# Fourier stage of a four-layer stack: other ticks for widenings, filters, back transforms and output products

## The reference

```python
x = einsum('bchw,oc->bohw', x, w_in)            # 64 -> 384 channels
xf = rfft2(8x8 patches of x) * fft_filter
x = irfft2(xf)                                  # back to pixels
x = depthwise_conv3x3(x, w_dw, padding=1)       # 9 taps per channel
x1, x2 = split(x, 2, axis=1)
x = einsum('bchw,oc->bohw', gelu(x1) * x2, w_out)   # 192 -> 64 channels
```

## Time and profile before

| | |
|---|---|
| median of three runs | 21086.46 us (21080.1 to 21098.46) |
| profiled execution, its own time | 21098.81 us |
| span of the profiled execution | 21097.0 us |
| first filter of the Fourier stage | 17206.8 us |
| last filter of the Fourier stage | 20572.2 us |
| busy in the span: VectorE, GpSimd, TensorE, ScalarE | 92%, 73%, 71%, 54% |

### The profile page before, as it was taken

One profiled execution on the slowest core, in us unless ns is written; L12 is line 12 of the kernel. 1 busy time (PEld: TensorE's weight loads), 2 busy tenths in 40 slices (PEclk: granted clock), 3 DMA queues, 4 the chain that ended last, 5 costly groups with the idle time before them and its releaser, 6 DMA issues. The chain is left out here.

```text
span 21097.0 us, 183109 instructions
## 1 busy us (share of the span) xinstructions
PE 14907.7 (71%) x47074; PEld 5387.9 (26%) x47074; DVE 19421.3 (92%) x12666; ACT 11474.3 (54%) x12716; POOL 15394.4 (73%) x6584
## 2 busy tenths in 40 slices
PE   4876666666666666666666666666666668888885
PEld 2331222222222222222222222222222224444444
DVE  5778999999999999999999999999999978888886
ACT  1115555555555555555555555555555546666663
POOL 3766777777777777777777777777777758888881
PEclk8887777777777777777777777777777779999997
DMA  3224444444444444444444444444444421111113
GB/s 117 95 90 112 111 114 116 111 113 116 114 109 116 115 112 114 115 112 112 114 117 110 114 116 110 114 116 114 109 116 114 111 63 30 30 30 30 30 26 132
DMA packets 574458, 2089.44 MB, mean 99 GB/s; under 512 B 70785, under 2 KB 88051, under 8 KB 550067
## 3 DMA queue, kind: packets, MB, share of 16 engines
q1 hardware_dynamic: 569122, 2081.45, 39.6%
q10 hardware_dynamic: 5265, 7.14, 0.1%
HBM read 856.39 MB, written 158.18 MB: 48 GB/s over the span
## 5 line engine op out<-in xcount | busy, mean ns | idle before, releaser
L1287 POOL TENSOR_TENSOR prod<-h,c_bc 128x1024 f32<-128x1024 f32 x4096 | 9571.1, 2350 | 4069.1 <-PE py L992 3088.1
L1246 DVE TENSOR_TENSOR_SCAN h<-da,state,px 128x1024 f32<-128x1024 f32 x4096 | 9613.4, 2347 | 193.2 <-DVE px L1239 24.6
L1133 ACT ACTIVATE da<-d_bc,a_neg 128x1024 f32<-128x1024 f32 x4096 | 4666.6, 1145 | 4670.2 <-DVE h L1246 4644.1
L1239 DVE TENSOR_TENSOR px<-px,du_bc 128x1024 f32<-128x1024 f32 x4096 | 5046.0, 1232 | 359.6 <-PE px L925 141.2
L925 PE MATMUL px<-cf,bsel 32*128 32x512 f32 x4096 | 3113.4, 899 | 3199.0 <-DVE h L1246 3198.9
L992 PE MATMUL py<-prod,ysel 128*32 128x512 f32 x16384 | 2725.9, 798 | 1560.0 <-POOL prod L1287 1560.0
L1874 POOL TENSOR_TENSOR acc<-acc,ta 128x1024 f32<-128x1024 f32 (+1 forms) x1040 | 2424.7, 2339 | 499.7 <-DVE acc L1774 370.1
L925 PEld LDWEIGHTS px<-cf,bsel 32*128 32x128 f32 x4096 | 957.5, 257 | 4989.4 <-DVE h L1246 4037.7
L1774 DVE SCALAR_TENSOR_TENSOR p_c<-zb,w_dw,p_c 128x1024 f32<-128x1024 f32 (+1 forms) x1560 | 1987.3, 1274 | 42.3 <-PE p_c L1546 9.8
L992 PEld LDWEIGHTS py<-prod,ysel 128*32 128x32 f32 x16384 | 511.2, 132 | 3808.6 <-POOL prod L1287 2800.9
L1673 ACT ACTIVATE ta<-zb,w_dw 128x1024 f32<-128x1024 f32 (+1 forms) x1040 | 1168.5, 1128 | 297.1 <-POOL acc L1874 275.5
(11 more groups left out here) (219 smaller groups left out, 18319.6 us busy)
## 6 DMA issues: line engine op xcount, KB each, us to landing
d_bc<-delta SPq DMA_DIRECT2D x1024, 512.0 KB, 8.1
du_bc<-du SPq DMA_DIRECT2D x1024, 512.0 KB, 7.7
c_bc<-c_rows_dram SPq DMA_DIRECT2D x1024, 512.0 KB, 4.0
hx<-x_dram SPq DMA_DIRECT2D x252, 256.5 KB, 4.8
st_x<-in_x_dram SPq DMA_DIRECT2D x32, 1024.0 KB, 4.8
ax<-in_x_dram SPq DMA_DIRECT2D x64, 512.0 KB, 3.4
xr<-x_dram SPq DMA_DIRECT2D x64, 512.0 KB, 6.0
x_dram<-xo SPq DMA_DIRECT2D x64, 512.0 KB, 5.3
```

What stands on the lines that cost most here:

```text
L1133: nc.scalar.activation(da[n % 4][:, :], d_bc[:, n % J, :], ACT.Exp, scale=a_neg[t.l][:, n:n + 1]).then_inc(da_done, 1)
L1239: nc.vector.tensor_tensor(out=x[:, :], in0=px[q % 2][:, :], in1=du_bc[:, j, :], op=ALU.mult).then_inc(m1_done, 1)
L1246: nc.vector.tensor_tensor_scan(h[:, n % 8, :], da[n % 4][:, :], x[:, :], state[:, 2 * t.l + t.b, n:n + 1], ALU.mult, ALU.add).then_inc(sca ...
L1287: nc.gpsimd.tensor_tensor(out=prod[j][:, :], in0=h[:, n % 8, :], in1=c_bc[q % 2][:, :], op=ALU.mult).then_inc(m2_done, 1)
```

## The change

The diff changes tick tables and the place of a few calls; no instruction is added or left out, and no wait is added or removed by hand.

```diff
--- before.py
+++ after.py
@@ -1426,14 +1426,14 @@
         TICKS = 24
         CONV_AT = {4 * (u - 1) + 1: u for u in range(1, 6)}
         NEXT_AT = 21
-        PROJECT_AT = (1, 4)
-        WIDEN_AT = {2 * p + 1: p for p in range(NP)}
-        BACK_AT = {j + 3: j for j in range(NJ)}
+        PROJECT_AT = (2, 5)
+        WIDEN_AT = {2 * p - 1: p for p in range(1, NP)}
+        BACK_AT = {j + 2: j for j in range(NJ)}
         TURN_AT = {4 * g + 7: g for g in range(NG)}
         FREQ_AT = {4 * g + 9: g for g in range(NG)}
-        CARRY_AT, GELU_BACK_AT, GELU_AT = 1, 5, 17
-        FILTER_N = {n: p for p, n in enumerate((3, 5, 8, 10, 13, 15, 18, 20))}
-        RESIDUAL_N, STATS_N = (3, 7), (4, 8)
+        CARRY_AT, GELU_BACK_AT, GELU_AT = 1, 6, 17
+        FILTER_N = {n: p for p, n in enumerate((1, 3, 6, 8, 11, 13, 16, 18))}
+        RESIDUAL_N, STATS_N = (5, 9), (6, 10)
 
         @block.sync
         def _(eng):
@@ -1582,8 +1582,6 @@
                 for j in range(TICKS):
                     if j in CONV_AT:
                         conv(s, b, CONV_AT[j])
-                    if not first and j in PROJECT_AT:
-                        project(s - 1, nb, r if rows_left else None, PROJECT_AT.index(j))
                     if not no_next:
                         if j in WIDEN_AT:
                             widen(ns, r + b, nb, WIDEN_AT[j])
@@ -1591,6 +1589,10 @@
                             from_freq(ns, BACK_AT[j])
                         if j == NEXT_AT:
                             conv(ns, nb, 0)
+                            if not no_row:
+                                widen(s + 2, r + 1, b, 0)
+                    if not first and j in PROJECT_AT:
+                        project(s - 1, nb, r if rows_left else None, PROJECT_AT.index(j))
                     if b == 0 and not no_row:
                         if j in TURN_AT:
                             turn(r + 1, TURN_AT[j])
@@ -1605,6 +1607,7 @@
                 for j in range(2 * p, 2 * p + 2):
                     from_freq(0, j)
             conv(0, 0, 0)
+            widen(1, 0, 1, 0)
             slot(0, 0, 0, first=True)
             slot(0, 1, 1)
             with pe.Fori(1, NR - 1) as r:
```

## The result

The changed kernel takes 21477.17 us (median of 4; 21474.63 to 21486.73) against 21090.99 for the kernel before: a ratio of 1.0184 (95% interval 1.0167 to 1.0202), +386 us. The forecast had the direction (+195) and not the size; 21477 lies 37 us above its range. The profiled execution took 21475.12.

What follows compares the result with a forecast made beforehand. VectorE was taken to set the pace, losing time to its filters' waits. Slots of 58.2 and 53.9 us make 112.1 against 105.8, +6.3 times 31 = +195, hence about 21280 us; range 21120 to 21440.

Steps and rivals of the forecast that it cites:

- walk: Step-by-step timing of two slots in the steady stage: 112.1 us against 105.8, +195 us in all; chance 0.6.
- T: VectorE's first tap of a slot, from which the forecast counts its times.
- wait for conv 5: End of the b = 0 slot: conv 5 ends at 51.6 for a VectorE ready at 51.3.
- Part 1: Widening 0 ahead: filter 0's wait goes (3.9 and 1.3); filter 1 waits 0.95 in b = 0.
- Part 2: Next wait lands at filter 3: T + 17.3 in b = 0, 16.9 in b = 1.
- Part 3: Projects later: TensorE idles 2.8 us behind project 1 for gelu and placement 3; filter 4 7.4 behind filter 3.
- part 4: Filters 5 to 7 by pitches: 5.0 and 8.2 us in b = 1; 5.9, 4.85 and 5.9 in b = 0.
- new buffer wait: Filter 3 also waits for back transform 3, behind its widening in the same tick: about 0.95 us a time.
- Half clock again: Rival: TensorE's clock falls behind the 2.8 us idle in each slot; 2.4 lost each, +149, 21430 us; chance 0.15.
- GpSimd's 22.3 us chain: From the end of unit 3 to GpSimd's first sum of unit 5, 22.3 us; placement 1 hangs on it.
- The stall is hidden: Rival: back transform 4 does not wait for the gelu; 2.8 less a slot, 21110 us, no change; chance 0.12.
- faster: Rival: about 3 us less in each slot's chain to filter 3, stall hidden too; -150, 20935 us; chance 0.13.

Runs made afterwards that it cites:

- e1: Changed kernel with three quarters of conv 2 repeated behind project 1, where TensorE idles for placement 3: 21312.24 us (ratio 1.0108 to the kernel before).
- e4: Kernel before with the early widening 0 alone, at tick 21 of the slot ahead: 20990.79 us (ratio 0.9954).
- e2: Changed kernel with ScalarE's late gelu one tick later (GELU_BACK_AT 6 becomes 7): 21246.16 us (ratio 1.0075 to the kernel before).
- e6: Kernel before with only the projects' part of the change (projects, late gelu, residuals and statistics later): 21421.91 us (ratio 1.0155).
- e5: Changed kernel with four buffers v instead of two: 21416.03 us (ratio 1.0154 to the kernel before).
- e3: Changed kernel with projects, late gelu, residuals and statistics back where they were before: 21079.95 us (ratio 0.9997 to the kernel before).

## Why the prediction was wrong

**Its walk held.** Step by step, in one b = 0 slot each (the two shown above), predicted against the changed kernel and against e1, which has no half clock behind the stall:

| step | predicted | changed kernel | e1_fill |
|---|---|---|---|
| filter 3 after T | 17.3 | 18.8 (conv 2 at reduced clock) | 17.1 |
| filter 3 to 4 | 7.4 | 8.6 | 7.4 |
| filter 4 to 5 | 5.9 | 6.3 | 5.9 |
| filter 5 to 6 | 4.85 | 4.85 | 4.85 |
| filter 6 to 7 | 5.9 | 5.9 | 5.9 |
| wait for conv 5 | 0.4 | 3.34 | 3.33 |

Not every slot is like these. In 16 of 24 b = 0 slots of the changed kernel conv 2 runs at full clock, filter 3 comes at T + 17.1, and filter 4 only 9.6 behind it. The two slots together show it best: 112.1 us forecast, 118.1 in the changed kernel and 112.7 in e1 (means of 23 and 25 pairs).

Part 1 was right: the wait at filter 0 went, and e4 shows the worth of that alone, 97 us. The 0.95 us put at filter 1 did not come: conv 1 took 3.16 us and not 3.78. Part 2 was right: filter 3 is where the next wait landed. Part 3 was right in place and size (2.76 for 2.8), and e2 and e6 show that the stall, with the clock behind it, is the main loss. In part 4 the pitches held wherever the clock was full; taking away the new buffer wait gave 61 us, a shift of the half clock included (e5).

**The step that failed is the clock.** The sum of part 3 carries the 2.8 us stall at its own length and has nothing for the clock behind it. "Half clock again" was put at 0.15, on the reading that the idle of 2.8 us "is nearer the short waits in what surrounds it". The trace of before has rows at both sides, a wait of 3.73 us with half clock behind it and waits of 1.2 us with none, and I let the shorter side decide. What the runs show in its place: 1.2 GHz behind the 2.76 us wait, and 165 us less (21477 to 21312) when the wait is filled. By the pair lengths that is 5.4 us a pair, or 2.7 us a slot.

The rival was also a little too small: it priced one stretch of half clock per slot at 2.4 us, +149, and left out conv 2 and conv 5. Conv 2, behind the restart of a slot and a placement wait of 1 us, runs at a lowered clock in 8 of 25 b = 0 slots (0.72, 4.62 us for 3.60), conv 5 in 15 of 25 (4.91 us for 3.60), with no single wait above 1.2 us ahead of it. The forecast's sum gives 21280 and e1 21312: of the error of 197 us, 165 are the clock behind the stall, as the fill shows, and the 32 left over are of the size of what the clock still costs at conv 5 in e1. No run tries that split.

Why the clock falls at conv 5 stays open. Widening 7 no longer stands between back transforms 11 and 12, and three back transforms in a row wait 1.18, 0.60 and 1.09 us ahead of it. But e2, e3 and e5 have the same order there, and their conv 5 is never slow. From back transform 6 to back transform 13, 18.8 us, the changed kernel and e3 do the same work with the same waits, at a clock of 1.00 in both; then the clock falls in one and not in the other. The order alone does not decide it.

The Trainium skill, "TensorE: Matmul & The Clock Gate", sections "HAM oscillation" and "A second HAM failure mode", tells of both forms: a wait in every round of a loop, and many small idles between groups of matmuls. The changed kernel's trace agrees, with 1.2 GHz behind the 2.76 us and a granted clock of 0.60 to 0.65 at conv 5. The trace of e3, with the same small waits ahead of conv 5 and a clock of 1.00, shows that they do not always bring it.

**Part of it was given back.** Where conv 5 makes the b = 0 slot end late, GpSimd's 22.3 us chain has run on meanwhile, and filter 3 of the next slot comes at T + 14.4 (19093.02 less 19078.59) in place of 16.9. So it is in 15 of 25 b = 1 slots. Against that, filter 4 follows 9.6 us behind filter 3 in these, in place of 7.4. In the mean the b = 0 slot takes 62.7 us where 58.2 was forecast, and the b = 1 slot 55.5 where 53.9 was.

**The rivals.** "The stall is hidden" was refuted by the 2.76 us; "faster" too, though the gain from the early waits exists by itself in e4. VectorE has no wait for SyncE's loads in the changed kernel's steady part, as forecast.

## What to carry to other kernels

When a producer is moved ahead in a hand-written order, look at what its old place covered: here project 1 moved from ahead of conv 2 to behind it, and TensorE no longer had conv 2 to do while ScalarE ran the gelu and the placement that TensorE needed next. Price such a stall with the slower clock behind it as well as with its own length, and ask of each in-order engine whether the operation that others wait for stands behind one that can wait. Test the parts one by one: of this change, one part alone gives 97 us, another alone takes 328, and a swap in ScalarE's order that the change did not touch gives 105 on top of the 97.

## What was not expected of the hardware

More work made the kernel faster: eight short matmul records (2.85 us) put into a 2.76 us wait took 165 us off the time, and the granted clock behind it stayed at 1.00 where it had fallen to between 0.50 and 0.66. And the clock fell without any long wait: in a stretch of five us of the changed kernel in which TensorE was busy for 3.4 and no wait was above 1.2, it was 0.60, and the 4.00 us behind it, all busy, ran at 0.65. The same work with the same waits ran at 1.00 in e3, and in the changed kernel itself only 15 of 25 such slots were slow at conv 5; what picks them is open:

```profile
19062.00:19067.00 5.00, 3.41 (x16) 3.01 (x17) 4.89 (x5) 3.83 (x6) 4.43 (x2) 0.60 0.00 0
```
